# Scores of two heads side by side, four more copies on ScalarE and another order of the first loads, in a four-layer kernel on one core

## The reference: what is computed

```python
x = layernorm(x + up(expert[dom](gelu(down(x)))))             # L0: adapter, expert chosen by id
y = ln(x) * (1 + scale(t)) + shift(t)                         # L1: a transformer block
q, k, v = heads(y @ Wq), heads(y @ Wk), heads(y @ Wv)         # 16 heads of 16
p = softmax(where(mask, -inf, q @ k.T / 4 + side))            # side: 16 x 16 x 256 x 256
y = y + (p @ v) @ Wo
y = y + gelu2(ln(y) @ W1) @ W2                                # F = 1024
z = layernorm(y + branch[kind](y))                            # L2: one of three small networks
out = max(z + dt * (-grad(A * z) + grad2(B * z) / 2), 0)      # L3: differences on a grid
```

## Time and profile before

| | before |
|---|---|
| median of 3 runs | 852.12 us (849.15 to 852.52) |
| the profiled execution | 850.75 us |
| its span | 849.0 us |
| TensorE, VectorE, ScalarE, GpSimd busy | 813.2, 737.0, 622.9, 163.3 us |
| copies of turned heads: ScalarE, VectorE | 178 x 603 ns, 78 x 684 ns |
| waits of TensorE for kl, for packings into ks | 3.8 us, 3.6 us |

### The profile page before, as it was taken

One profiled execution on the slowest core, in us unless ns is written; L12 is line 12 of the kernel. 1 busy time (PEld: TensorE's weight loads), 2 busy tenths in 40 slices (PEclk: granted clock), 3 DMA queues, 4 the chain that ended last, 5 costly groups with the idle time before them and its releaser, 6 DMA issues.

```text
span 849.0 us, 18721 instructions
## 1 busy us (share of the span) xinstructions
PE 813.2 (96%) x6029; PEld 697.4 (82%) x6029; DVE 737.0 (87%) x2472; ACT 622.9 (73%) x1286; POOL 163.3 (19%) x160
## 2 busy tenths in 40 slices
PE   8788899999999999999999999999999999999985
PEld 5665688889888888888888888988888888887874
DVE  7767767989989898998989898998989899878777
ACT  5257787978787887878788797878788787677551
POOL 2210122220402112120312222040211222111020
PEclk9889999999999999999999999999999999999998
DMA  7979786685756677676758878676768867475110
GB/s 226 202 205 220 163 203 157 157 200 139 171 161 172 166 160 189 164 184 142 188 155 178 166 161 198 143 173 157 177 158 176 177 166 181 114 174 143 51 32 25
DMA packets 147626, 137.33 MB, mean 162 GB/s; under 512 B 19314, under 2 KB 144819, under 8 KB 147524
## 3 DMA queue, kind: packets, MB, share of 16 engines
q1 hardware_dynamic: 145668, 134.99, 66.1%
q10 hardware_dynamic: 1856, 1.07, 0.8%
HBM read 98.23 MB, written 4.23 MB: 121 GB/s over the span
## 4 chain that ended last, share of the span: by engine, by line
PE 85%; DVE 7%; issue 2%; DMA 2%; ACT 2%; ACTq 1%; POOL 1%; POOLq 0%; DVEq 0%
PE turn_bank L1429 13%; PE back_bank L1473 12%; PE context_bank L1483 7%; PE score_bank L1686 7%; PE score_bank L1687 6%; PE front_bank L1467 5%; PE attend_bank L1467 5%; PE back_bank L1467 5%; PE back_bank L1453 3%; PE back_bank L1444 3%; PE attend_bank L1453 3%; PE front_bank L1522 3%; PE front_bank L1802 3%; PE attend_bank L1401 2%; DMA ks<-kl 2%
## 5 line engine op out<-in xcount | busy, mean ns | idle before, releaser
L594 ACT ACTIVATE sc<-sc,negmax 128x256 f32<-128x256 f32 x512 | 231.7, 505 | 20.0 <-DVE negmax L1290 18.6
L1290 DVE CUSTOM_DVE_ANT_0 sc<-score_bank,side 128x256 f32<-128x256 f32 x512 | 195.4, 420 | 35.6 <-PE score_bank L1687 26.4
L588 ACT ACTIVATE pt<-turn_bank 128x512 f32<-128x512 f32 x178 | 107.2, 603 | 126.4 <-PE turn_bank L1429 105.4
L1429 PE MATMUL turn_bank<-ident,sc 128*128 128x128 f32 x1024 | 157.1, 277 | 1.8 <-ACT sc L594 1.7
L1429 PEld LDWEIGHTS turn_bank<-ident,sc 128*128 128x128 f32 x1024 | 123.5, 142 | 32.5 <-issue 13.7
L1686 PE MATMUL score_bank<-ks,qs 128*128 128x256 f32 x512 | 122.9, 322 | 4.4 <-DMA ks<-kl 3.6
L1473 PE MATMUL back_bank<-w,ffT 128*128 128x256 f32 x480 | 111.1, 379 | 0.0
L508 POOL TENSOR_TENSOR rstd<-var,half_neg 128x2 f32<-128x2 f32 x64 | 50.9, 795 | 274.5 <-DVE var L1014 266.8
L1687 PE MATMUL score_bank<-mask_neg,ident_r 128*128 128x512 f32 x256 | 102.3, 400 | 0.0
L1473 PEld LDWEIGHTS back_bank<-w,ffT 128*128 128x128 f32 x480 | 90.9, 190 | 11.8
L1686 PEld LDWEIGHTS score_bank<-ks,qs 128*128 128x128 f32 x512 | 78.6, 193 | 13.0 <-issue 6.6
(11 more groups left out here) (298 smaller groups left out, 1974.7 us busy)
## 6 DMA issues: line engine op xcount, KB each, us to landing
side<-in_side SPq DMA_DIRECT2D x128, 512.0 KB, 5.7
qs<-qh SPq DMA_DIRECT2D x128, 64.0 KB, 4.4
qs<-ql SPq DMA_DIRECT2D x128, 64.0 KB, 4.5
ks<-kh SPq DMA_DIRECT2D x120, 64.0 KB, 4.2
ks<-kl SPq DMA_DIRECT2D x120, 64.0 KB, 4.5
wb<-in_wb SPq DMA_DIRECT2D x15, 512.0 KB, 7.3
xN<-in_x SPq DMA_DIRECT2D x16, 256.0 KB, 5.3
wc<-in_wc SPq DMA_DIRECT2D x16, 256.0 KB, 2.9
```

The costliest lines, as they stand in the source:

```text
L588: e.activation(pt[:, h % NP2, :, :], two(tbank[h % 2]), ACT.Copy).then_inc(copied[h % 4], 1)
L594: i = e.activation(sc[:, h % NS, q, :], sc[:, h % NS, q, :], ACT.Exp, bias=negmax[:, q, h:h + 1], scale=-1.0)
L1290: i = e.tensor_tensor_reduce(sc[:, s % NS, q, :], two(sbank[s % 2])[:, q, :], side[:, (H * X.i + s) % NSIDE, q, :], -1.0, 3.4e38, ALU.add, ...
L1429: i = e.transpose(tbank[h % 2][:, k * S + q * P:k * S + q * P + P], sc[:, h % NS, q, k * P:k * P + P], ident[:, :])
```

## The change

It has four parts.

1. The scores of heads s and s + 1 are both computed at the start of an even slot s; odd slots begin without one. The work of a slot behind the scores stays in its slot.
2. In slots 3 and 11 the four transposes come ahead of the slot's fp32r products (`differ`, the first feed-forward piece); before they came behind.
3. `ACT_COPIES` gains 5, 6, 11 and 12. In batch 0 the list stays what it was. VectorE keeps slot 10 (and 11 and 12 in batch 0).
4. SyncE's list: the two loads of grid_A move from slot 1 to slot 8 of batch -1; the five of `load_rows` (d1T, d2T, b2, gamma3, beta3) from slot 3 to slot 13 of batch 0; of the sixteen packings for heads 8 to 15 of sample 0 the last eight move from slot 9 of batch -1 to slot 3 of batch 0, behind `load_ada`, which waits for x1 of the next sample.

```diff
-ACT_COPIES = (0, 1, 2, 3, 4, 7, 8, 9, 13, 14, 15)
-FIRST_ACT_COPIES = ACT_COPIES + (5, 6)
+ACT_COPIES = (0, 1, 2, 3, 4, 5, 6, 7, 8, 9, 11, 12, 13, 14, 15)
+FIRST_ACT_COPIES = (0, 1, 2, 3, 4, 5, 6, 7, 8, 9, 13, 14, 15)
...
-                load(ld_grid, (t_a[:, :, :], tall(d["grid_B"][0])), (t_b[:, :, :], tall(d["grid_B"][1])), (t_c[:, :, :], tall(d["grid_B"][2])),
-                     (x2[:, :, :], tall(d["grid_A"][0])), (x3[:, :, :], tall(d["grid_A"][1])))
+                load(ld_grid, (t_a[:, :, :], tall(d["grid_B"][0])), (t_b[:, :, :], tall(d["grid_B"][1])), (t_c[:, :, :], tall(d["grid_B"][2])))
...
+            def load_grid_a():
+
+                load(ld_grid, (x2[:, :, :], tall(d["grid_A"][0])), (x3[:, :, :], tall(d["grid_A"][1])))
...
-            later = {(-1, 1): load_early, (0, 3): load_rows, (0, 7): lambda: load_w2(0), (0, 11): lambda: load_w2(1), (0, 15): load_wa}
+            later = {(-1, 1): load_early, (-1, 8): load_grid_a, (0, 13): load_rows, (0, 7): lambda: load_w2(0), (0, 11): lambda: load_w2(1), (0, 15): load_wa}
...
-                    if t == -1 and s == 9:
-                        e.wait_ge(ev["ql_ready"], F.n)
-                        e.wait_ge(ev["kl_ready"], F.n)
-                        e.wait_ge(pool_set, KS_SET)
-                        for b in range(NBLK):
-                            for u in range(2):
-                                pack_k(e, 1, b, u)
-                                pack_q(e, 1, b, u)
+                    for t0, s0, blocks_ in ((-1, 9, (0, 1)), (0, 3, (2, 3))):
+                        if is_step(t, s, t0, s0):
+                            e.wait_ge(ev["ql_ready"], 1)
+                            e.wait_ge(ev["kl_ready"], 1)
+                            e.wait_ge(pool_set, KS_SET)
+                            for b in blocks_:
+                                for u in range(2):
+                                    pack_k(e, 1, b, u)
+                                    pack_q(e, 1, b, u)
...
+            def score(x, h):
+
+                head(e, biased, x, h - 2)
+                for q in range(TT):
+                    e.matmul(two(sbank[h % 2])[:, q, :], qs[:, h // 2, q * P:q * P + P], ks[:, h, :], start=(q == 0), stop=False)
+                i = e.matmul(sbank[h % 2][:, :], ident_r[:, :], mask_neg[:, x.par, :, :], start=False, stop=True)
+                i.then_inc(scored[h % 4], 1)
...
-                    if X:
+                    if X and s % 2 == 0:
                         if s % HM == 0:
                             e.wait_ge(ld_stack[s // HM], times(X, STACKED))
-                        head(e, biased, X, s - 2)
                         if s == 0:
                             e.wait_ge(ev["mask_ready"], X.n)
...
+                        score(X, s)
+                        score(X, s + 1)
...
+                        four(flip)
                         if U:
                             differ(U, 1)
-                            four(flip)
...
                     elif s == 11:
+                        for n in range(4):
+                            flip(n)
                         if B:
                             wait(e, ev["x4_ready"], B.p)
                             e.wait_ge(ev["n3l_ready"], B.n)
                             project_T_parts(bbank, w1, w1l, 0, n3h, n3l, 2, ev["w1_done"])
-                        for n in range(4):
-                            flip(n)
```

More of the change, by code:

```diff
@@ L1677, in body @@
                         e.wait_ge(ld_late, 8 * 16)
-                    if X:
+                    if X and s % 2 == 0:
                         if s % HM == 0:
                             e.wait_ge(ld_stack[s // HM], times(X, STACKED))
-                        head(e, biased, X, s - 2)
                         if s == 0:
                             e.wait_ge(ev["mask_ready"], X.n)
-                        for q in range(TT):
-                            e.matmul(two(sbank[s % 2])[:, q, :], qs[:, s // 2, q * P:q * P + P], ks[:, s, :], start=(q == 0), stop=False)
-                        i = e.matmul(sbank[s % 2][:, :], ident_r[:, :], mask_neg[:, X.par, :, :], start=False, stop=True)
-                        i.then_inc(scored[s % 4], 1)
+                        score(X, s)
+                        score(X, s + 1)
                     flip = no_more
@@ L1722, in body @@
                             turn(bbank, x3, ev["x3_turned"])
+                        four(flip)
                         if U:
                             differ(U, 1)
-                            four(flip)
-                        else:
-                            for n in range(4):
-                                flip(n)
                     elif s == 4:
```

## The result

| | before | changed |
|---|---|---|
| median | 852.32 us (4 runs, 849.15 to 853.12) | 875.46 us (4 runs, 875.00 to 876.52) |
| the profiled execution | 850.75 us | 875.47 us |
| its span | 849.0 us | 873.7 us |
| copies of turned heads: ScalarE, VectorE | 178, 78 | 238, 18 |

The ratio is 1.028, with a 95% interval of 1.0259 to 1.030: slower, as forecast, by 23 us where 18 were expected (869.9 us; the range was 851 to 880). The forecast's sum starts from the profiled execution of the kernel before, so its terms (19.1 us) are best held against the two spans, which differ by 24.7 us.

The account below looks back on a forecast made before the run. TensorE, busy 96% of the span and waiting for nobody in the steady part, was taken as the bound. The profiled 850.75 us + 17.0 (steady part) + 0.6 + 1.5 (loads) gave 869.9 us, range 851 to 880.

Parts of the forecast that it names:

- A: Slot 9: the turn of xN waits for ScalarE's copy of the v product, +0.38 us in 14 batches.
- B: Slot 12: the second score waits for VectorE's reading of head 11, 0.44 us in 15 batches.
- C: Slot 13: the up product waits for ScalarE's g1, +0.45 us in 13 batches.
- The loops priced at 0: Other loops out of TensorE and back: margins of at least 0.1 to 0.2 us, so no cost.
- Passages: Six of 16 fp32-to-fp32r passages a batch go away on TensorE: 0.05 us a batch saved, 0.8 in all.
- rival 1: Each fp32-to-fp32r passage costs 0.085 us and the new waits don't come: 844.7 us, 5%.
- Term (3): 896 KB of loads now in slot 13 delay the first score of batch 1: +1.5 us, between 0 and 3.9.
- term (2): Batch 0: eight packings behind SyncE's wait for x1 put the v product at 60.6, not 60.01: +0.6 us.
- term (1): Two grid_A loads leave the stretch before the first score: 0 us, ends -2.0 and +1.
- 3 (only A): Only A comes; idle time of ScalarE and VectorE may absorb B and C: 857.4 us, 9%.
- 4 (VectorE the pacemaker at every even slot): Second scores wait 0.15 us in each of eight slots, 1.2 us more in 15 batches: 888 us, 5%.
- 2 (the start decides): Moved loads remove 2.0 and 3.8 us of waiting and 2.5 of half clock, A to C absent: 842.4 us, 6%.

Follow-up runs that it names:

- experiment 6: The changed kernel with score 9 back in slot 9, the other pairs kept: 868.15 us, ratio 1.0187.
- experiment 7: The changed kernel with score 13 back in slot 13: 875.19 us, ratio 1.0274.
- experiment 10: The changed kernel with the copy of slot 10 on ScalarE too: 879.46 us, ratio 1.0324.
- experiment 2: The kernel before with SyncE's new load order, but the five loads of load_rows back in slot 3 of batch 0: 851.69 us, ratio 0.9999.
- experiment 1: The kernel before with only SyncE's loads in the new order: 851.51 us, ratio 0.9996.
- experiment 4: The kernel before with only the copies of slots 5, 6, 11 and 12 moved to ScalarE from batch 1 on: 861.45 us, ratio 1.0116.
- experiment 8: The changed kernel with the copy of slot 11 back on VectorE: 871.60 us, ratio 1.0228.
- experiment 3: The kernel before with only the scores of two heads side by side in even slots: 876.58 us, ratio 1.0295.
- experiment 11: The changed kernel with scores 9, 11 and 13 back in their own slots and the copy of slot 11 back on VectorE: 858.14 us, ratio 1.0077.
- experiment 12: The changed kernel with score pairs only from batch 3 on, each score in its own slot before: 872.27 us, ratio 1.024.
- experiment 9: The changed kernel with the copy of slot 12 back on VectorE, slot 11's kept on ScalarE: 875.96 us, ratio 1.028.

## Why the forecast held, and where it was off

**The rule it rested on.** TensorE waited for nobody in the steady part, so every new wait is paid once a batch. It held: 16.8 of the 24.7 us are in batches 3 to 13, at 1.53 us each.

**A.** Forecast 0.38 us in 14 batches, measured 0.47. Right in cause (experiment 6), short by the handover: I had 0.05 us from ScalarE's end to TensorE's start, from VectorE's kl; it was 0.14.

**B.** Forecast 0.44 us in 15 batches, measured 0.41 and 0.10 for the slower restart of the score. Its cause, VectorE's reading behind the low part of n3, is where TensorE waits, but experiments 7 and 10 show that taking B away gains nothing while C is there.

**C.** Forecast 0.45, measured 0.44 with its restart. The distance from the turn of n3 that I had worked out for g1, 9.22 us, is 9.21 in the trace, and it moved as a queue should: 8.85 without the copy of slot 11, 9.20 without that of slot 12, 9.70 with that of slot 10. That "their sum is safer than either" was the right way to put it. C came in batch 0 too, for which I had not counted it, and B did not come in batch 1, for which I had.

**The loops priced at 0.** One was not: D, 0.10 to 0.12 us a batch, from part 2. I had counted part 2's passages and not asked what `differ` delivers later. The sentence on the margins named slot 6's context for the copy of slot 5. It never waited in the steady part; in the last sample it did, 1.3 us, so this margin was gone in one place where I had priced it at 0.

**Passages.** -0.05 us a batch forecast, about 0 measured. The reading that neighbours only shift time from row to row held; rival 1's 0.085 a passage is out.

Together the period is short by 0.31: 0.09 + 0.07 - 0.01 + 0.11 + 0.05, that is handover and restarts, D, and the passages. That makes 3.4 us over batches 3 to 13.

**The loads.** +2.1 us forecast, +0.1 measured. Term (3) was near (1.5 for 1.15, as far as the 1.15 are the loads', experiment 2). The v product of batch 0 came at the forecast time, by errors that cancelled (experiment 1), but term (2) put +0.6 on it and left out the clock, whose part (I had up to 2.5) turned out to be 1.5 us of gain; so the sign of the term was wrong, inside its ends. Of term (1), the grids, no run shows more than the spread of the first score between profiles: 37.1 to 38.4 us in the ten with the grids moved, 37.3 to 40.2 in the four without. The means, 37.7 and 38.8, hint at a gain of about 1 us, which four profiles can't show.

**The ends of the pipeline.** In batches 0 to 2 the errors cancelled, 4.7 us measured for 4.9: the loads 0.1 for 2.1, the pairs 2.8 for 2.0, copies and transposes 1.9 for 0.9. That this sum was right is luck. From batch 14 on I had 0.8 us left and 2.8 came. That step, taking the last batches for steady ones with A and C absent, is the second part of the miss: a copy or a pair costs more where less other work stands around it, 1.3 us at one place (experiment 4). The miss of 5.6 us is thus 3.4 in batches 3 to 13, 2.0 from batch 14 on, 0.4 ahead of the first score, which is within its spread, and -0.2 in batches 0 to 2.

**The rivals.** 3 (only A) is out, since C stands by itself in experiment 4 and B in experiment 8. 4 (VectorE the pacemaker at every even slot) is out in the steady part: 0.6 us more on VectorE cost 0.08 (experiment 8). Its mechanism is real in the first and last batches, and in slot 0 when VectorE keeps its copies (experiment 3). 2 (the start decides) was right that the start gains from the packings, but by 1 us in batch 0, not 8.

**A better version.** None was found. The changed kernel without A to C is still 0.8% slower than the one before, and of the parts only the moved packings and grids gave anything, 1.7 us in a profile, which the timing (0.9999) doesn't confirm. Two things were not tried. One is the move in slot 11 without that in slot 3. The other is in ScalarE's queue between the turn of n3 and g1: 2.56 of its 8.68 us are two loads of activation tables (1.28 us each, from 444.89 and 446.77 us in the kernel before).

## What to carry to other kernels

Where one engine is the bound and waits for nobody, a reorder that takes no work from it can only lose, unless it shortens a wait that exists: list what each moved instruction stood in front of, follow every short loop out of the engine and back, and compare times in the trace. Count waits that hang on one start once, by the distance from it to the last consumer, since removing one of them feeds the next. And when work is given to an engine with idle time, look at what stands behind it in that queue: the copy of slot 11 cost 0.4 us a batch, that of slot 12, of the same length, nothing.

## What the runs showed of the hardware

- After a wait TensorE loses 0.06 to 0.1 us beyond it. A score pair that begins after a stop takes 0.34 us to its mask instead of 0.24, an up product 0.97 instead of 0.91, and the fp32 turn of xN started 0.14 us after ScalarE's copy ended, where 0.05 to 0.06 is seen for kl, the reading and g.
- A stop can cost more than its own length. In batch 0, after 3.8 us of idle, TensorE ran the next 6 us at a mean granted clock of 0.54; after two stops of 0.6 and 1.3 us it ran them at 1.00, which gained 1.5 us behind the stop. The length of the stop alone does not tell: over the next 6 us the clock was granted at 0.72 after a stop of 1.66 us (91.1 us, experiment 1) and after one of 1.76 us (794.3 us, experiment 11), and at 1.00 after one of 2.17 us (55.3 us, experiment 12).
- In the first 100 us the clock is not the same from profile to profile, even where the order of the work is: from 36 to 52 us the mean granted clock is 0.57 in the changed kernel, 0.79 in experiment 7 and 0.89 in experiment 9. A microsecond in batches 0 to 2 of one profile proves little.
- Loads that nobody waits for at once delay others: with 896 KB issued from 70.8 to 74.7 us, the first score of batch 1 waited 1.1 to 2.3 us for its packings in nine profiles, without them 0 to 1.4 in five.
